# Three linear-attention loops rebuilt: v from TensorE into three PSUM banks, multiplied in place and scanned there

## The chip, the cores and the metric

The kernel runs on one core of a Trainium2 chip. The metric is the device time of one execution in microseconds (us), as the median of several runs; lower is better.

## The reference

A residual model of eight layers over x of 2048 tokens by 128 channels, all in f32: each layer adds its block's output to x, and each block works on the layer-normed x.

```
x = x + softmax_attention(norm(x))      # 16 heads of 8, causal, over 2048 tokens
x = x + channel_mix(norm(x))
x = x + gated_linear(norm(x))           # the three "linear" blocks
x = x + channel_mix(norm(x))
x = x + retention(norm(x))
x = x + experts(norm(x))                # top 2 of 8
x = x + lightning(norm(x))
x = x + experts(norm(x))
```

The three linear blocks have one form. For each head (16) and each pair (d, e) of its 8 by 8 state there is a recurrence over the tokens, and the output is a sum over d:

```
S[t] = a[t] * S[t-1] + k[t, d] * v[t, e]
o[t, e] = sum over d of q[t, d] * S[t]
```

In gated a is sigmoid(key) per channel and token, k is 1 - a, and the output goes through the matrix ho with a bias. In retention and lightning a is a constant per head; retention then normalises per head over time and multiplies by ro; lightning takes silu of q, k and v, normalises per token, multiplies by a gate (two small products and a sigmoid) and by lo.

## The kernel before

The stages run one after another: softmax_attention, channel_mix, linear_attention("gated"), channel_mix, linear_attention("retention"), experts, linear_attention("lightning"), experts. x stays in SBUF with tokens on partitions (16 tiles of 128); xT holds the normed and transposed x, channels on partitions.

**A linear stage** has 128 partitions for (head, d) and loops over n = 0..31: four chunks c of 512 tokens (NC, CH), and in each the eight values e (HD). A step n makes the row of v for e, replicated over d, in the layout (head, d) x 512; multiplies it by k (L1120, DVE) into one of four SBUF buffers upd; scans it (L1134, DVE) with the decay into a state buffer; multiplies the state by q (L1085, POOL) into z; and TensorE adds z into the output bank of the chunk (add_product, four steps later by LAG). In gated and lightning add_product uses z as the stationary operand, four 128-token tiles at a time, with reduce_w (L1229), and the output comes with tokens on partitions; for gated reduce_w is orep, the output matrix's rows replicated by eight DMAs, so that the output matrix is applied in the same product. In retention it is one product with pick stationary (L1224), and the output has channels on partitions.

The rows of v come in two ways. For all e of the first chunk and five of eight later, TensorE makes them (L1244) into one of two PSUM banks (4 and 5); in lightning ACT applies Silu in place (L1185). For e = 3, 5 and 7 of the later chunks (by_dma) TensorE makes the whole of v for the chunk once (L1250), ACT copies it (L1190), SP stores it to DRAM and loads it back replicated, and POOL multiplies it by k (L1090), three steps ahead. At step 5 of a chunk k and q of the next chunk are projected (L1213, two products). Lightning also makes a gate at steps 2 and 3 (L1256, L1259). DVE adds the finished chunk to x in gated (add: L1096, L1098 and the statistics L194) or takes statistics of y.

Each engine's queue runs in the order of the code; semaphores carry the dependencies.

**The softmax stage** has an order written out by a planner, attention_order, which counts time for each engine and yields PLAN. The maxima of the scores (DVE L720 over TensorE products L771 into a ring of two slots, banks 4 to 7) are computed ahead of the exponentials (ACT L841 over products L788 into three score banks 0 to 2) and the products with v (L802, bank 3). For each of the 16 steps (four heads, 512 queries) the maxima are turned (L824), copied to mrow (L733), and written by four small DMAs (set_maxima, L659) as rows of the stacked Q; the scores of that step wait for them. ACT issues these DMAs for the first four steps (EARLY), SP for the rest. SP also stores the bf16 parts of Q and K of each chunk to DRAM and loads them stacked (store, stack), chunks 2 and 3 right at the start of this block. A "fill" is a product into a free ring slot whose result is not used; the planner puts one in where PE would wait over 0.25 us by its count, if the ring slot is free.

## Time and profile before

| | |
|---|---|
| median of 3 runs | 1269.7 us (1269.53 to 1271.92) |
| profiled execution, its time | 1268.4 us |
| its span, first to last instruction | 1266.7 us |
| mean granted TensorE clock | 0.871 of full |
| busy: PE, DVE, ACT, POOL | 989.5, 873.5, 511.3, 479.7 us |

The profile is of one execution. PE is TensorE (PEld its weight loads), DVE VectorE, ACT ScalarE, POOL GpSimd, SP the queue that issues DMAs. L1134 is line 1134 of the kernel before. A busy PE is not a PE at its peak, as matmuls are pipelined. An f32 product shows as two MATMUL instructions. Idle time of an engine that is not the limit costs nothing, so the rows are read stage by stage.

### The profile page before, as it was taken

The page shows a single profiled execution, that of the slowest core. Times are in us where ns is not written, and L with a number is a line of the kernel's source. Part 1 is how long each engine was busy: PE and PEld are TensorE (multiplying, and loading weights), DVE is VectorE, ACT ScalarE, POOL GpSimd, SP SyncE. Part 2 cuts the span into 40 slices and gives each one's busy share as a digit, 9 for nine tenths or more (in the row PEclk, how much of TensorE's full clock was granted, in tenths as well). Part 3 has the DMA queues.
Part 4 walks back from the last instruction along what each step waited for, and adds up shares of the span by engine and source line. Part 5 has one row for each costly group of instructions (what it writes and reads, how often), then busy time and mean ns, then how long its engine had stood idle before and what let it go on. Part 6 is the DMA issues. An engine that isn't in the chain of part 4 may idle for free. (4 is left out here: it accounts for less than half of the span.)

```text
span 1266.7 us, 17452 instructions
## 1 busy us (share of the span) xinstructions
PE 989.5 (78%) x5892; PEld 500.1 (39%) x5892; DVE 873.5 (69%) x1502; ACT 511.3 (40%) x1048; POOL 479.7 (38%) x506
## 2 busy tenths in 40 slices
PE   5477899899999999686767775399984985369994
PEld 3222222222222333544453223166661544236663
DVE  6957889898988830889878985633337997643335
ACT  5234577687877776320021101033334321113333
POOL 2311110011101112248834883146642797136662
PEclk9657889899999999789868986599996997679997
DMA  6881000000000000511001101011112110101114
GB/s 134 175 192 19 1 1 1 1 1 2 1 1 1 2 3 7 193 58 51 9 1 33 51 17 33 13 32 42 43 37 75 59 34 1 34 21 42 43 43 116
DMA packets 50204, 51.45 MB, mean 41 GB/s; under 512 B 7668, under 2 KB 39804, under 8 KB 50108
## 3 DMA queue, kind: packets, MB, share of 16 engines
q1 hardware_dynamic: 44888, 40.06, 12.4%
q0 software_dynamic: 4992, 10.23, 3.0%
q8 instruction: 51, 0.84, 0.3%
q14 instruction: 33, 0.27, 0.1%
q10 hardware_dynamic: 240, 0.05, 0.0%
HBM read 33.22 MB, written 16.91 MB: 40 GB/s over the span
## 5 line engine op out<-in xcount | busy, mean ns | idle before, releaser
L720 DVE TENSOR_REDUCE mpart<-ps 128x2 f32<-128x1024 f32 (+3 forms) x320 | 325.3, 1061 | 59.4 <-PE ps L771 34.2
L841 ACT ACTIVATE arena<-ps 128x512 f32<-128x512 f32 (+3 forms) x640 | 292.1, 542 | 143.2 <-PE ps L788 133.9
L788 PE MATMUL ps<-arena 51*128 51x512 bf16 (+3 forms) x640 | 182.3, 372 | 14.9 <-ACT arena L841 6.2
L1085 POOL TENSOR_TENSOR arena<-arena 128x512 f32<-128x512 f32 x96 | 148.6, 1559 | 64.9 <-DVE arena L1134 63.7
L771 PE MATMUL ps<-arena 51*128 51x512 bf16 (+3 forms) x640 | 149.9, 383 | 21.2 <-DVE mpart L720 15.7
L802 PE MATMUL ps<-arena,w 128*32 128x512 f32 (+3 forms) x1280 | 160.5, 575 | 2.9 <-ACT arena L841 2.5
L690 POOL TENSOR_SCALAR_AFFINE_SELECT arena<-arena 128x512 f32<-128x512 f32 x64 | 40.6, 634 | 313.8 <-ACT arena L841 231.3
L1669 ACT ACTIVATE arena<-ps 128x512 f32<-128x512 f32 x78 | 46.6, 597 | 219.6 <-PE ps L1732 163.4
L1579 DVE COPY arena<-ps 128x128 f32<-128x128 f32 x78 | 22.8, 292 | 154.4 <-PE ps L1722 146.5
L1134 DVE TENSOR_TENSOR_SCAN arena<-cst,arena 128x512 f32<-128x512 f32 x64 | 124.0, 1959 | 2.0 <-POOL arena L1090 2.0
L788 PEld LDWEIGHTS ps<-arena 51*128 51x128 bf16 x640 | 50.2, 95 | 174.5 <-ACT arena L841 136.4
L1634 POOL DMA_INDIRECT results<-arena x78 | 76.8, 984 | 91.5 <-DVE arena L1596 77.2
L1623 POOL DMA_INDIRECT arena<-tokens,arena x78 | 75.7, 971 | 76.7 <-DVE arena L1572 53.5
L1731 PE MATMUL ps<-w,arena 128*128 x156 | 82.9, 614 | 2.9 <-DVE arena L1579 2.4
L1750 PE MATMUL ps<-w,arena 128*128 x624 | 82.7, 275 | 1.1 <-DVE arena L1596 1.1
L1732 PE MATMUL ps<-w,arena 128*128 x156 | 81.4, 604 | 0.0
L1750 PEld LDWEIGHTS ps<-w,arena 128*128 128x128 f32 x624 | 75.8, 192 | 1.6 <-issue 1.5
L1244 PE MATMUL ps<-xt,arena 128*128 128x512 f32 x138 | 72.7, 615 | 3.5 <-DVE arena L1120 3.4
L182 PE MATMUL ps<-cst,xn 128*128 128x128 f32 x96 | 22.5, 396 | 60.7 <-DVE xn L165 58.9
L173 POOL TENSOR_TENSOR small<-small,neghalf 128x4 f32<-128x4 f32 x32 | 32.4, 1050 | 96.2 <-DVE small L160 96.2
L1120 DVE TENSOR_TENSOR arena<-ps,arena 128x512 f32<-128x512 f32 x69 | 46.0, 667 | 28.9 <-PE ps L1244 19.2
L189 ACT COPY xt<-ps 128x512 f32<-128x512 f32 x28 | 16.2, 589 | 121.5 <-PE ps L182 121.4
(263 smaller groups left out, 1525.6 us busy)
## 6 DMA issues: line engine op xcount, KB each, us to landing
w<-in_w SPq DMA_DIRECT2D x2, 2048.0 KB, 11.4
arena<-results SPq DMA_DIRECT2D x16, 256.0 KB, 4.9
arena<-q_stack SPq DMA_DIRECT2D x8, 384.0 KB
arena<-k_stack SPq DMA_DIRECT2D x8, 384.0 KB
arena<-g_v SPq DMA_DIRECT2D x9, 256.0 KB
arena<-r_v SPq DMA_DIRECT2D x9, 256.0 KB, 3.6
arena<-l_v SPq DMA_DIRECT2D x9, 256.0 KB, 3.6
tokens<-arena SPq DMA_DIRECT2D x8, 256.0 KB, 2.4
```

The source lines that it names most:

```text
L720: nc.vector.tensor_reduce(out=mpart[:, 2 * pl:2 * pl + 2, t, kc], in_=ps[:, bank:bank + 2, 0:width], axis=AX.X, op=ALU.max).then_inc(ring_ ...
L771: ins = nc.tensor.matmul(ps[:, bank + side, 0:width], rows(Qs, side, 2 * g + pl, (c * TPC + t) * P, (c * TPC + t + 1) * P), rows(Ks, side, ...
L788: nc.tensor.matmul(ps[:, n % ST, off:CH], rows(Ks, j % 2, 2 * g + j // 2, kt * P, (kt + 1) * P), rows(Qs, j % 2, 2 * g + j // 2, c * CH + ...
L802: ins = nc.tensor.matmul(ps[32 * j:32 * j + 32, O, off:CH], vg[kt // (NT // 2)][:, kt % (NT // 2), g * GH + j, :], probs[:, u % 2, j, off: ...
L841: nc.scalar.activation(probs[:, n % 2, j[0], off:CH], ps[:, (GH * n + j[0]) % ST, off:CH], ACT.Exp, scale=float(HD) ** -0.5).then_inc(exp_ ...
L1085: nc.gpsimd.tensor_tensor(z[:, n % ZB, :], state[:, n % SB, :], q[:, c % 2, :], ALU.mult).then_inc(z_ready, 1)
L1134: nc.vector.tensor_tensor_scan(out=state[:, n % SB, :], data0=a, data1=upd[n % UB], initial=0.0 if c == 0 else state[:, (n - HD) % SB, CH ...
L1623: nc.gpsimd.indirect_dma_start(out=xs[:, s, :], out_offset=None, in_=token_rows, in_offset=bass.IndirectOffsetOnAxis(ap=gather_row[:, s:s ...
L1634: nc.gpsimd.indirect_dma_start(out=result_rows, out_offset=bass.IndirectOffsetOnAxis(ap=result_row[:, s:s + 1], axis=0), in_=y[:, s % YB, ...
L1731: nc.tensor.matmul(ps[:, i % 2, :], xsT[:, i % 2, :], w1[:, expert[i], :], start=True, stop=True)
L1732: nc.tensor.matmul(ps[:, 2 + i % 2, :], xsT[:, i % 2, :], w3[:, expert[i], :], start=True, stop=True).then_inc(up_ready, 1)
L1750: ins = nc.tensor.matmul(ps[:, 7, 0:D], hidT[:, s % 2, f, :], w2[:, expert[s], f, :], start=f == 0, stop=f == NF - 1)
```

## The change

In the linear stages all rows of v are made by TensorE, into three PSUM banks (4, 5, 0). DVE multiplies by k in place in the bank, and the scan reads its input from the bank. The way over DRAM, POOL's updates, orep and the upd buffers are gone. The sum over d is one product with pick stationary in all three kinds, with channels on partitions; in gated and lightning ACT copies the chunk's sum (copy_inner), TensorE turns it to tokens on partitions (outer: with ho as the moving operand in gated, as transposes in lightning), into the same bank, and in lightning ACT copies it again (copy_outer). In gated the add moves from step 5 to step 7. Norm uses banks 1 and 7.

In the softmax stage SP issues all row DMAs; store and stack of chunks 2 and 3 come after the rows of steps 1 and 3 have landed; and the planner also puts fills into a free score bank.

```diff
@@ attention_order
-                while can[what][0] - pe > 0.25 and free <= pe:
+                n = GH * su + sj
+                bank_free = n < GH * NU and (n < 3 or exp_end[n - 3] + 0.06 <= pe) if n < 3 or len(exp_end) > n - 3 else False
+                while can[what][0] - pe > 0.25 and (free <= pe or bank_free):
...
-                    plan.append(("fill", slots))
+                    plan.append(("fill", slots) if free <= pe else ("fill scores", n))
@@ softmax_attention, sync
                         stack(sp, 1)
-                        for c in (2, 3):
-                            store(sp, c)
-                            stack(sp, c)
-                        for k in range(EARLY, NS):
+                        for k in range(NS):
                             set_maxima(sp, k)
+                            if k in (1, 3):
+                                c = (k + 3) // 2
+                                for j in range(GH):
+                                    sp.wait_ge(max_set[j], 16 * (k + 1))
+                                store(sp, c)
+                                stack(sp, c)
@@ softmax_attention, tensor
+                        def fill_scores(n):
+                            if n >= ST:
+                                pe.wait_ge(exp_done, n - ST + 1)
+                            nc.tensor.matmul(ps[:, n % ST, 0:320], identb[:], cstb[:, 0:320], start=True, stop=True)
@@ softmax_attention, scalar
-                            if what == "turn max" and n < EARLY:
-                                set_maxima(act, n)
@@ linear_attention
-            norm = Norm(name, x, xn, NT, 1e-5)
+            norm = Norm(name, x, xn, NT, 1e-5, banks=(1, 7))
+            def v_bank(n):
+                return ps[:, (4, 5, 0)[n % 3], :]
@@ gpsimd
-                        if n + 3 in by_pool:
...
-                            nc.gpsimd.tensor_tensor(upd[u % UB], vd[:, m % VB, :], k[:, u // HD % 2, :], ALU.mult).then_inc(upd_pooled, 1)
@@ vector
-                        nc.vector.tensor_tensor(upd[n % UB], v_in, k[:, n // HD % 2, :], ALU.mult).then_inc(upd_ready, 1)
+                        nc.vector.tensor_tensor(v_bank(n), v_bank(n), k[:, n // HD % 2, :], ALU.mult).then_inc(upd_ready, 1)
...
-                            out=state[:, n % SB, :], data0=a, data1=upd[n % UB],
+                            out=state[:, n % SB, :], data0=a, data1=v_bank(n),
...
-                        if kind == "gated" and c >= 1 and n % HD == LAG + 1:
+                        if kind == "gated" and c >= 1 and n % HD == HD - 1:
                             add(dve, c - 1)
@@ scalar
+                def copy_inner(act, c):
                     act.wait_ge(z_used, (c + 1) * HD)
+                    if kind == "retention":
+                        nc.scalar.copy(y[:, c * CH:(c + 1) * CH], ps[:, 6 + c % 2, :]).then_inc(sum_out, 1)
+                    else:
+                        if c >= 2:
+                            act.wait_ge(outer_ready, c - 1)
+                        nc.scalar.copy(inner[:, c % 2, :], ps[:, 6 + c % 2, :]).then_inc(inner_out, 1)
+                def copy_outer(act, c):
+                    act.wait_ge(outer_ready, c + 1)
                     nc.scalar.copy(y[:, c * CH:(c + 1) * CH], ps[:, 6 + c % 2, :]).then_inc(sum_out, 1)
...
-                            nc.scalar.activation(dec[:, c % 2, :], pk, ACT.Sigmoid, bias=col["key_b"])
...
-                            nc.scalar.activation(k[:, c % 2, :], pk, ACT.Sigmoid, bias=negb, scale=-1.0).then_inc(kq_out, 1)
+                            nc.scalar.activation(k[:, c % 2, :], pk, ACT.Sigmoid, bias=negb, scale=-1.0)
+                            nc.scalar.activation(dec[:, c % 2, :], pk, ACT.Sigmoid, bias=col["key_b"]).then_inc(kq_out, 1)
@@ tensor
+                        nc.tensor.matmul(ps[:, 6 + c % 2, :], pick[:, e, :], z[:, n % ZB, :], start=e == 0,
+                                         stop=e == HD - 1).then_inc(z_used, 1)
+                    def outer(c):
+                        pe.wait_ge(inner_out, c + 1)
+                        for t in range(TPC):
+                            out, tile = ps[:, 6 + c % 2, t * P:(t + 1) * P], inner[:, c % 2, t * P:(t + 1) * P]
+                            if kind == "gated":
+                                ins = nc.tensor.matmul(out, tile, w["ho"][:], start=True, stop=True)
+                            else:
+                                ins = nc.tensor.transpose(out, tile, ident)
+                        ins.then_inc(outer_ready, 1)
...
+                        if n >= 3:
+                            pe.wait_ge(scanned, n - 2)
+                        nc.tensor.matmul(v_bank(n), vrep[:, e].rearrange("p h d -> p (h d)"),
+                                         xT[:, c * CH:(c + 1) * CH], start=True, stop=True).then_inc(v_ready, 1)
...
+                        if e == LAG + 2 and c >= 1 and kind != "retention":
+                            outer(c - 1)
```

## Rows read from the trace of the kernel before

**Rows 1.** Windows, the three loops: busy us (instructions) per engine, PE clock, DMA share, GB/s
```profile
550.40:635.80 85.40, 65.26 (x302) 43.43 (x301) 78.92 (x70) 7.16 (x12) 63.20 (x40) 0.91 0.12 37
680.70:763.40 82.70, 63.31 (x121) 23.30 (x120) 75.79 (x58) 7.10 (x12) 64.89 (x40) 0.89 0.13 39
976.90:1059.20 82.30, 68.26 (x317) 41.76 (x315) 76.76 (x67) 24.33 (x42) 66.76 (x40) 0.96 0.13 39
```

**Rows 2.** Timeline of DVE: start, us, line, idle before; start and end of retention's loop
```profile
609.22 0.84 DVE L194 BATCH_NORM_STATS2 stats<-x 128x6 f32<-128x128 f32 x4
...
682.13 1.21 DVE L1134 TENSOR_TENSOR_SCAN arena<-cst,arena 128x512 f32<-128x512 f32 x1
683.26 0.67 DVE L1120 TENSOR_TENSOR arena<-ps,arena 128x512 f32<-128x512 f32 x1
683.85 1.92 DVE L1134 TENSOR_TENSOR_SCAN arena<-cst,arena 128x512 f32<-128x512 f32 x1
...
761.17 2.27 DVE L1134 TENSOR_TENSOR_SCAN arena<-cst,arena 128x512 f32<-128x512 f32 x1 [0.51 <-POOL arena L1090]
768.10 0.69 DVE L1106 BATCH_NORM_STATS2 stats<-arena 128x6 f32<-128x512 f32 x1 [4.67 <-ACT arena L1150]
```

**Rows 3.** Timeline of POOL, the same stretch
```profile
683.43 1.27 POOL L1085 TENSOR_TENSOR arena<-arena 128x512 f32<-128x512 f32 x1 [5.13 <-DVE arena L1134]
```

**Rows 4.** Instructions of one line: duration ns min/median/max, first and last start
```profile
L1120 DVE TENSOR_TENSOR arena<-ps,arena x69: 658/659/693, 550.4 to 1050.3; 128x512 f32<-128x512 f32 x69
...
L1098 DVE TENSOR_TENSOR x<-x,out_bias x4: 691/844/1446, 586.6 to 641.3; 128x512 f32<-128x512 f32 x4
```

**Rows 5.** Timeline of PE, products back to back in gated and in retention
```profile
561.56 1.02 PE L1244 MATMUL ps<-xt,arena 128*128 128x512 f32 x2
...
562.43 1.05 PE L1229 MATMUL ps<-arena 128*128 128x128 f32 x8
...
687.44 1.02 PE L1224 MATMUL ps<-arena,cst 128*128 128x512 f32 x2
688.29 1.02 PE L1213 MATMUL ps<-xt,w_rk 128*128 128x512 f32 x2
```

**Rows 6.** Timeline, hand-over from DVE to PE (gated), from PE to ACT (lightning)
```profile
562.74 0.66 DVE L1120 TENSOR_TENSOR arena<-ps,arena 128x512 f32<-128x512 f32 x1
...
563.46 1.12 PE L1244 MATMUL ps<-xt,arena 128*128 128x512 f32 x2
...
983.70 1.02 PE L1244 MATMUL ps<-xt,arena 128*128 128x512 f32 x2
...
984.76 0.58 ACT L1185 ACTIVATE ps<-ps 128x512 f32<-128x512 f32 x1 [1.17 <-PE ps L1244]
```

**Rows 7.** Timeline of ACT, the issues of the second set of rows
```profile
76.05 3.07 ACTq L659 DMA_DIRECT2D arena<-mrow  x4
79.22 2.13 ACT L841 ACTIVATE arena<-ps 128x256 f32<-128x256 f32 x8 [4.95 <-issue]
```

**Rows 8.** Timelines: SP, first store and last stack issue of chunk 2; DVE, fourth set
```profile
57.69 4.27 SPq L375 DMA_DIRECT2D q_stack<-w  x6
...
72.53 0.62 SPq L383 DMA_DIRECT2D arena<-k_stack  x1
...
118.92 0.18 DVE L726 TENSOR_REDUCE negmax<-mpart 128x16 f32<-128x32 f32 x1
```

**Rows 9.** Windows in the softmax stage, columns as in rows 1
```profile
50.00:100.00 50.00, 33.54 (x276) 12.72 (x274) 34.12 (x47) 15.00 (x38) 7.48 (x20) 0.59 0.87 185
100.00:115.00 15.00, 12.88 (x82) 3.71 (x80) 11.35 (x14) 5.83 (x12) 0.00 (x0) 0.54 0.00 1
...
125.00:135.00 10.00, 8.26 (x56) 2.33 (x56) 5.78 (x6) 6.18 (x16) 1.27 (x2) 0.66 0.00 1
...
170.00:220.00 50.00, 46.85 (x390) 14.30 (x386) 46.34 (x47) 37.41 (x83) 5.86 (x12) 1.00 0.01 2
```

**Rows 10.** Window in gated's loop, columns as in rows 1
```profile
575.00:580.00 5.00, 1.88 (x10) 1.79 (x10) 5.00 (x4) 0.00 (x0) 5.00 (x3) 0.87 0.22 56
```

More of the change, by code:

```diff
@@ L1010, in linear_attention @@
             k = take(2 * CH).rearrange("p (b t) -> p b t", b=2)
-            spare = take(2 * CH)
-            dec = spare.rearrange("p (b t) -> p b t", b=2)
-            upd = take(2 * CH)
             SB, ZB = HD + 4, HD
@@ L1018, in linear_attention @@
             vrep = take(HD * P).rearrange("p (e h d) -> p e h d", e=HD, h=H)
-            orep = take(HD * P).rearrange("p (e m) -> p e m", e=HD)
+            inner = take(2 * CH).rearrange("p (b t) -> p b t", b=2)
             y = take(T)
@@ L1023, in linear_attention @@
             g1 = low_rank[0:HD, :].rearrange("p (b t) -> p b t", b=2)
-            UB = 4
-            upd = [half[:, i * CH:(i + 1) * CH] for half in (upd, low_rank if kind == "gated" else spare) for i in (0, 1)]
             negb = take(1)
-            VB = 4
-            vd = take(VB * CH).rearrange("p (b t) -> p b t", b=VB)
-            v_full = xn[:, 0:2 * TPC, :].rearrange("p (b t) d -> p b (t d)", b=2)
-            v_dram = nc.dram_tensor(name + "_v", [NC, P, CH], FP32, kind="Internal").ap()
-            by_dma = [n for n in range(NC * HD) if n >= HD and n % HD in (3, 5, 7)]
-            by_pe = [n for n in range(NC * HD) if n not in by_dma]
-            by_pool, by_dve = by_dma, by_pe
-            v_full_ready = sem(name + "_v_full_ready")
-            v_full_out = sem(name + "_v_full_out")
-            v_stored = sem(name + "_v_stored")
-            v_loaded = [sem(f"{name}_v_loaded{b}") for b in range(VB)]
-            norm = Norm(name, x, xn, NT, 1e-5)
+            norm = Norm(name, x, xn, NT, 1e-5, banks=(1, 7))
+            dec = take(2 * CH).rearrange("p (b t) -> p b t", b=2)
+            def v_bank(n):
+                return ps[:, (4, 5, 0)[n % 3], :]
             rep_ready = sem(name + "_rep_ready")
```

104 lines of the change are left out of this document (25 added, 79 removed).

## Prediction

> **What bounds the kernel now.** I read the page's busy shares first; no engine is full over the whole span, so the question is which one is full in each stage. The table of windows gives it. In the softmax stage's steady part, 170 to 220 us, PE is busy 46.9 and DVE 46.3 of 50 us [rows 9]; in the loops of the three linear stages DVE is busy 78.9 of 85.4, 75.8 of 82.7 and 76.8 of 82.3 us [rows 1]. The change rewrites these loops, 250.4 us together; it also edits the softmax stage.
>
> Then the timeline of DVE in the loop of retention [rows 2]. The first scan, with POOL idle, takes 1.21 us (1.13 to the next start); from the second on a scan takes 1.92. The reader is to see why: the multiply at 683.26 gives way to a scan at 683.85, but POOL's first z product runs from 683.43 to 684.70 [rows 3], and from 684.70 the scan needs its 1.1 us more, to 685.77. So a scan (two SBUF inputs) stands still while POOL's product (two SBUF inputs) runs, and one step costs 0.58 + 1.85 = 2.43 us. The multiply L1120, with one input in PSUM, takes 658 to 693 ns in all 69 cases, beside POOL or not [rows 4]. L1098, with both inputs in SBUF, goes from 691 to 1446 ns. That is the pattern on which the whole forecast rests: only an operation of DVE with two SBUF inputs is held by POOL, and the scan's held part is 0.7 us, 96 times.
>
> PE's timeline gives the next limit. One 128x512 f32 product is two instructions and keeps PE for 0.87 us (561.56 to 562.43) or 0.85 us (687.44 to 688.29) at full clock [rows 5].
>
> **The change, part by part.**
>
> *Scan from PSUM.* Its data1 moves to PSUM, so one SBUF input stays (dec or the constant). By the pattern it takes 1.13 start to start; with the 0.59 of the multiply a step is 1.73 instead of 2.43. No row shows a scan that reads PSUM, nor a DVE write into PSUM. Bounds: nothing extra (the multiply's read from PSUM costs no more than L1098's free 691 ns), or 0.3 us a step for both instructions together, half of a multiply again, an estimate at the far end. I take nothing, as the multiply is the nearest row; 0.3 would be 29 us over 96 steps. The Trainium skill ("VectorE: DVE Perf Modes", section on the TRN2 errata) speaks against this: it gives a VectorE instruction from PSUM 62 cycles more than one from SBUF. By that the scans alone would add about 6 us; the rows of L1120 and L1098 do not show it.
>
> *POOL without the updates.* Three products in eight from the second chunk on leave POOL. Its z product (1.27 us) then fits into 1.73, so POOL's lag, for which the last scan waited, goes. Eight rows of v by PE in place of five, no copy of v to DRAM and back, no ACT copy of v: off the path, except that PE gets the work.
>
> *PE becomes the neighbour limit.* Per step it does one product for v and one for the sum: 2 x 0.86 = 1.72 us, against DVE's 1.73. Its extras therefore show: k and q (1.72 per chunk, three chunks), in gated the four final products (8 instructions, 0.9), in lightning the two gate products (1.72) and four transposes (0.6, estimate). The slack: from a bank's release to its next multiply is 0.06 (563.40 to 563.46) + 1.12 + 0.04 (984.72 to 984.76, to ACT) = 1.22 us [rows 6], and three banks allow 1.73, so 0.5 us of PE's lateness is free. In lightning ACT's Silu stands between: PE start to Silu start 1.06, Silu 0.58 [rows 6], so the chain is 0.16 + 1.06 + 0.58 + 0.04 = 1.84 us (0.16: the release and the 0.1 that a waiting product takes longer). The multiply n waits for the scan n-3 by this chain and the scan n-1 follows it after 1.73, so two steps take at least 1.84 + 1.73, one 1.78.
>
> Chunks of eight steps, 13.8 us by DVE:
> - Retention: first chunk 13.8 + (1.72 - 0.5) = 15.0; the middle two also the statistics (0.6) = 15.6; last 14.4 (no k and q). Sum 60.6 against 82.7: minus 22.1.
> - Gated: the add of a chunk is DVE time (0.66 + 0.69 + 0.8 of statistics [rows 2, 4] = 2.15). First 15.0; middle: between PE's sum 13.8 + 2.6 = 16.4 and all extras in a row 18.3, I take 17.2; last 16.4. Sum 65.8 against 85.4: minus 19.6.
> - Lightning: PE bound, 20 products x 0.86 + 0.6 = 17.8, with 0.3 of friction 18.1 in the middle, 17.4 first, 16.4 last. Sum 70.0 against 82.3: minus 12.3.
>
> *Tails.* Retention: from the last scan's end to the last statistics is 768.79 - 763.44 = 5.4 us now, as POOL is three products behind; afterwards 0.1 + 1.27 (z, [rows 3]), 1.18 (sum), 0.63 (ACT's copy, as the Silu), 0.7 (statistics): 3.9. Minus 1.4. Gated and lightning gain as much and lose most of it to the added turn: a copy, and four products or transposes with a second copy (1.2 to 1.9 us, less the 8 small matmuls that one matmul pair replaces). I take 0.5 each. Together minus 2.4.
>
> Sum of the linear stages: 22.1 + 19.6 + 12.3 + 2.4 = 56.4 us. Bounds: by DVE alone (62, 57, 58 us) 76; with scans still held by POOL (2.43 a step) only the removed waits, 9.
>
> *Order of k and dec, Norm's banks, the loads of orep*: the two sigmoids come as a pair either way; banks 1 and 7 are free then; orep loads beside the norm. Nothing on the path; without that cover it would be one sigmoid, some 0.7 us.
>
> *Softmax stage: row DMAs from SP.* Now ACT issues the first four sets. 76.05 to 79.12 it issues four DMAs, its exponentials start at 79.22 after 4.95 us without work [rows 7], and PE and DVE wait with it. These sixteen issues move to SP. Behind SP's new waits stand store and stack of chunks 2 and 3 (28 DMAs): chunk 2's maxima are first wanted after the fourth set is reduced, at 119.1 us; its store can start once the second set has landed, near 80, and store and stack take SP 57.69 to 73.15 = 15.5 us [rows 8], with landing some 20. That is 19 us of cover, about 10 when the stage runs faster. In exchange the small row loads no longer share the queues with the bulk stores. DVE is busy 34.1 of 50 us between 50 and 100, against 46.3 at 170 to 220 [rows 9]: at most 12 us to win. I take 6.
>
> *Fills into the score banks.* At 100 to 115 and 125 to 135 PE's clock is at 0.54 and 0.66, that is largely at 1.2 GHz, after gaps in its work; by the 0.927 share of 170 to 220 DVE lost 2.6 and 3.5 us there [rows 9], and two such stretches follow before 235. Fills keep PE at work in such gaps. Some 10 us are at stake, part of it the ACT gaps; I take 4. None, or plus 3 if fills stand in front of maxima, is the other end. The planner's order may shift with them; I keep it as neutral.
>
> Sum: 1268.4 (profiled, its span 1266.7 and 1.7 around it) - 56.4 - 6 - 4 = 1202.0. The median of the runs is 1.3 above the profiled time: **1203 us**.
>
> **Rivals.**
> - *PSUM is dearer for DVE* (0.3 us a step): 1203 + 29 = 1232. Against it: 658 ns of L1120. For it: no row shows a PSUM write by DVE or a scan from PSUM. Chance 0.14.
> - *The scan stays held by POOL*: it writes SBUF, reads dec or the constant and its start value from SBUF. Then the linear stages give 9, in all 1203 + 47 = 1250. Against it: L1120 writes SBUF too and is never held. The Trainium skill ("SBUF — State Buffer", section Who interferes with whom) says that a DVE instruction with at most one SBUF input outside the two-port modes doesn't contend; by that this rival is out. Chance 0.08.
> - *The softmax stage gives nothing or loses*, since chunk 2's stack comes late or fills stand in the way: 1213 to 1216. Chance 0.10.
> - *The other side: PE at 1.2 GHz in the loops.* Its waits between banks let the clock fall, as between 575 and 580 us, where PE had 1.88 us of work in 5 and the clock was 0.87 [rows 10]. At 1.2 GHz a step is 4 x 0.86 = 3.44 us, PE bound, 1.7 more than 1.73. It outweighs all the gain when 66 / 1.7 = 39 of the 96 steps run so; with 45 the time is 1279. Against it: PE would be 99% loaded, and at 170 to 220, with 46.9 of 50 busy, the clock is 1.00. Chance 0.06.
> - The forecast: 0.62.
>
> **How the numbers follow.** A measurement of this kernel tells about 0.2% from no change. All cases but the last end more than 0.2% below 1269.7: faster 0.93, same 0.01, slower 0.06. The likeliest case's own range is 1185 to 1218 (linear stages 45 to 65, softmax 3 to 18). The range asked for must reach the dearer PSUM case and stays short of the held scan: 1182 to 1236.
>
> **What the profile will show.** Right: scans near 1.2 us beside a running POOL; a DVE step of 1.7 to 1.8; PE near 100% at clock 1.0 in the loops, and DVE's waits now for the v product at the fifth to sixth step of each chunk; in lightning waits for ACT's Silu; loops of about 61, 66 and 70 us; no ACT issue gap near 76 us, and fills between 100 and 240. Wrong: scans of 1.9 (held), multiplies over 0.75 (PSUM write), PE clock under 0.8 in the loops, DVE waiting for a stack DMA near 110 us. Most of my risk is in the PE extras: if they overlap DVE's slack better than I count, gated and lightning gain up to 10 us more.

## The result, and the profile after it

The changed kernel takes 1202.2 us (median of 4 runs, 1197.0 to 1205.2) against 1269.6 us (1267.3 to 1271.9) before; the ratio is 0.9465, 95% interval [0.9424, 0.9506]. It is faster by 5.3%. The forecast was 1203 us. The profiled execution took 1200.0 us, its span is 1198.2 us (before 1266.7).

Each stage's norm begins with the same DVE instruction, so its starts split the 68.5 us of span that went: up to the first channel mix 513.2 became 497.8 (minus 15.4), the gated stage 102.8 became 84.0 (minus 18.8), retention with its own norm 111.6 became 90.3 (minus 21.3), lightning up to its output norm 100.2 became 87.7 (minus 12.5), and the rest, mixes and experts, gave 0.5. So the linear stages brought 52.6 us, where the forecast had 56.4, and the softmax stage 15.4, where it had 10.

The windows of the three loops in the changed kernel, from the first multiply to the end of the last scan (they answer to [rows 1]):

```profile
533.90:601.10 67.20, 61.70 (x158) 27.13 (x158) 60.92 (x73) 7.08 (x13) 39.18 (x31) 1.00 0.00 1
646.40:709.00 62.60, 59.74 (x135) 24.35 (x136) 58.43 (x67) 5.32 (x9) 39.35 (x31) 1.00 0.00 1
919.90:991.30 71.40, 69.52 (x162) 26.22 (x160) 59.84 (x73) 29.30 (x51) 39.17 (x31) 1.00 0.00 0
```

DVE's busy time fell from 78.9, 75.8 and 76.8 us to 60.9, 58.4 and 59.8, and POOL's from 63 to 67 to 39. PE is now busy 92, 95 and 97% of the loops, and its granted clock is 1.00 in all three: the rival with the slow clock did not come.

The start of retention's loop, the timelines of DVE and then of POOL (they answer to [rows 2, 3]):

```profile
648.09 1.21 DVE L1112 TENSOR_TENSOR_SCAN arena<-cst,ps 128x512 f32<-128x512 f32 x1
649.21 0.67 DVE L1098 TENSOR_TENSOR ps<-ps,arena 128x512 f32<-128x512 f32 x1
649.80 1.21 DVE L1112 TENSOR_TENSOR_SCAN arena<-cst,ps 128x512 f32<-128x512 f32 x1
```

```profile
649.38 1.27 POOL L1072 TENSOR_TENSOR arena<-arena 128x512 f32<-128x512 f32 x1 [5.62 <-DVE arena L1112]
```

POOL's z product runs from 649.38 to 650.65, over most of the scan that starts at 649.80. In the kernel before, that scan took 1.92 us; here it takes 1.21, as the one before it with POOL idle. A step is 649.80 - 648.09 = 1.71 us in the first chunk. The groups of instructions, with shapes kept apart, give the means for the whole kernel:

```profile
L1098 DVE TENSOR_TENSOR ps<-ps,arena 128x512 f32<-128x512 f32 x96 | 65.6, 684 | 33.0 <-PE ps L1229 17.2 <-ACT ps L1171 15.6
L1112 DVE TENSOR_TENSOR_SCAN arena<-cst,arena,ps 128x512 f32<-128x512 f32 x48 | 60.9, 1271 | 0.0
L1112 DVE TENSOR_TENSOR_SCAN arena<-arena,ps 128x512 f32<-128x512 f32 x32 | 40.0, 1254 | 0.0
```

The multiply that writes into PSUM takes 684 ns on the mean (before 667, into SBUF). A scan has one of two lengths: 1.21 in the first chunk, 1.27 from the second on, where its start value is a column of the state and not 0.0. And 33 us of idle time stand before the multiplies, 17.2 behind the v product of PE and 15.6 behind ACT's Silu. What was DVE's own time before is now in part waiting for its neighbours. One such wait in retention, on DVE and on PE:

```profile
686.48 1.27 DVE L1112 TENSOR_TENSOR_SCAN arena<-cst,arena,ps 128x512 f32<-128x512 f32 x1
688.86 0.70 DVE L1098 TENSOR_TENSOR ps<-ps,arena 128x512 f32<-128x512 f32 x1 [1.11 <-PE ps L1229]
```

```profile
686.08 1.02 PE L1196 MATMUL ps<-xt,w_rk 128*128 128x512 f32 x2
686.94 1.02 PE L1196 MATMUL ps<-xt,w_rq 128*128 128x512 f32 x2
687.80 1.02 PE L1229 MATMUL ps<-xt,arena 128*128 128x512 f32 x2
```

The projections of k and q keep PE for 687.80 - 686.08 = 1.72 us; the v product behind them is late, and DVE waits 1.11 us. Retention has such a wait in each of three chunks (1.31, 1.34, 1.11 us). The gated loop has the same three, two more of 0.73 behind the outer products, and smaller ones, 6.2 us together. Lightning has fifteen waits for the Silu, 11.4 us together. These are 21.8 of the 33.0 us; the other 11.1 stand ahead of the three loops (3.4, 3.5 and 4.3), where DVE waits for the first row of v.

The softmax stage, by windows (they answer to [rows 9]; the last takes in the rest of the stage, which in the kernel before had DVE 254.7 and a clock of 0.95):

```profile
50.00:100.00 50.00, 38.44 (x353) 16.36 (x353) 38.77 (x53) 13.76 (x36) 7.53 (x20) 0.84 0.63 128
100.00:115.00 15.00, 13.86 (x94) 4.04 (x96) 10.46 (x11) 10.61 (x21) 0.07 (x1) 0.74 0.01 1
125.00:135.00 10.00, 9.58 (x79) 3.02 (x77) 8.61 (x10) 8.32 (x17) 0.95 (x2) 1.00 0.66 157
170.00:220.00 50.00, 45.97 (x369) 15.27 (x369) 46.93 (x51) 30.87 (x70) 6.73 (x16) 1.00 0.01 2
160.00:450.00 290.00, 275.22 (x2260) 86.44 (x2257) 249.39 (x272) 219.21 (x469) 30.94 (x79) 0.99 0.01 2
```

The clock in the first three of these windows is higher than before (0.84, 0.74 and 1.00 against 0.59, 0.54 and 0.66), and DVE does 38.8 us of its work between 50 and 100 instead of 34.1. ACT has no issues and no 4.95 us hole at 76 us any more. But there is a new hole, on PE. The timeline of SP, and of PE:

```profile
88.44 0.60 SPq L385 DMA_DIRECT2D arena<-q_stack  x1
...
92.21 27.94 SPq L660 DMA_DIRECT2D arena<-mrow  x8
```

```profile
94.93 0.31 PE L819 MATMUL ps<-cstb,identb 128*128 128x320 bf16 x1
100.83 1.03 PE L792 MATMUL ps<-arena 51*128 51x512 bf16 x3 [5.58 <-DMA arena<-mrow]
```

SP issues the four loads of chunk 2's stack from 88.44 on (384 KB each), and the small rows of set 2 right behind them, from 92.21 on (the line takes set 3's in as well). PE waits 5.58 us for these rows, and the window after the hole is the one with the clock at 0.74.

### The profile page after: what moved, and what is told of

Read it like the earlier page. It is cut to its first block and busy times, and to the rows that moved or that the text cites. A ratio compares the mean times of both kernels' runs of the same rounds, so it can differ in the third digit from the quotient of the medians.

```text
span 1198.2 us, 17070 instructions
## 1 busy us (share of the span) xinstructions
PE 979.1 (82%) x5703; PEld 468.7 (39%) x5703; DVE 823.8 (69%) x1529; ACT 514.6 (43%) x1056; POOL 400.7 (33%) x479
## 5 line engine op out<-in xcount | busy, mean ns | idle before, releaser
L792 PE MATMUL ps<-arena 51*128 51x512 bf16 (+3 forms) x640 | 175.0, 356 | 13.3 <-DMA arena<-mrow 6.0
L806 PE MATMUL ps<-arena,w 128*32 128x512 f32 (+3 forms) x1280 | 153.4, 551 | 2.7 <-ACT arena L852 2.2
L1072 POOL TENSOR_TENSOR arena<-arena 128x512 f32<-128x512 f32 x96 | 121.8, 1269 | 91.9 <-DVE arena L1112 85.1
L775 PE MATMUL ps<-arena 51*128 51x512 bf16 (+3 forms) x640 | 140.8, 359 | 12.9 <-DVE mpart L724 5.8
L1598 POOL DMA_INDIRECT results<-arena x78 | 77.0, 987 | 90.5 <-DVE arena L1560 77.1
L1229 PE MATMUL ps<-xt,arena 128*128 128x512 f32 x192 | 99.9, 604 | 8.1 <-DVE arena L1112 7.3
L1204 PE MATMUL ps<-arena,cst 128*128 128x512 f32 x192 | 98.8, 599 | 3.6 <-POOL arena L1072 3.3
L1098 DVE TENSOR_TENSOR ps<-ps,arena 128x512 f32<-128x512 f32 x96 | 65.6, 684 | 33.0 <-PE ps L1229 17.2
L1714 PEld LDWEIGHTS ps<-w,arena 128*128 128x128 f32 x624 | 75.8, 192 | 1.5 <-issue 1.5
L182 PE MATMUL ps<-cst,xn 128*128 128x128 f32 x96 | 22.3, 393 | 60.9 <-DVE xn L165 59.2
L1112 DVE TENSOR_TENSOR_SCAN arena<-cst,arena,ps 128x512 f32<-128x512 f32 x48 | 60.9, 1271 | 0.0
## 6 DMA issues: line engine op xcount, KB each, us to landing
w<-in_w SPq DMA_DIRECT2D x2, 2048.0 KB, 11.1
```

Of the source, the lines that this page charges most:

```text
L775: ins = nc.tensor.matmul(ps[:, bank + side, 0:width], rows(Qs, side, 2 * g + pl, (c * TPC + t) * P, (c * TPC + t + 1) * P), rows(Ks, side, ...
L792: nc.tensor.matmul(ps[:, n % ST, off:CH], rows(Ks, j % 2, 2 * g + j // 2, kt * P, (kt + 1) * P), rows(Qs, j % 2, 2 * g + j // 2, c * CH + ...
L806: ins = nc.tensor.matmul(ps[32 * j:32 * j + 32, O, off:CH], vg[kt // (NT // 2)][:, kt % (NT // 2), g * GH + j, :], probs[:, u % 2, j, off: ...
L1072: nc.gpsimd.tensor_tensor(z[:, n % ZB, :], state[:, n % SB, :], q[:, c % 2, :], ALU.mult).then_inc(z_ready, 1)
L1204: nc.tensor.matmul(ps[:, 6 + c % 2, :], pick[:, e, :], z[:, n % ZB, :], start=e == 0, stop=e == HD - 1).then_inc(z_used, 1)
L1229: nc.tensor.matmul(v_bank(n), vrep[:, e].rearrange("p h d -> p (h d)"), xT[:, c * CH:(c + 1) * CH], start=True, stop=True).then_inc(v_read ...
```

## The experiments

All ran beside the kernel before. Where two experiments are compared, I use the loops (first multiply to end of the last scan) of their profiles: in kernels with the changed loops these agree within 0.15 us where the code of a loop is the same and the clock is 1.00. The start of the first channel mix does not: nine kernels with the same softmax code as the changed one (497.8) have it between 493.6 and 500.0 us, one profile of each. So a start of the mix is good to about 3 us, and totals that differ by less say little by themselves.

### The softmax part alone

The linear stages are those of the kernel before; only the edits to the planner, the fills, the row DMAs and the order of store and stack are made.

> The kernel before with the softmax part of the change alone (fills in the score banks, all row DMAs on SP, stores and stacks put between them); the linear stages are those of before. Theory: the two parts don't touch each other, so the first channel mix begins at 498 us as in the changed kernel instead of 513, and everything after it stays as it was: 1254 us, 15 under before. Rival: part of the gain ahead of the mix is owed to something else, or is paid back later: 1260 to 1270.

Measured: 1252.6 us, ratio 0.9849 [0.9834, 0.9864]; the mix begins at 498.2, and the loops are 85.4, 82.0 and 83.4 us where they were 85.4, 82.8 and 82.3: retention 0.8 shorter, lightning 1.1 longer. That goes with PE's mean clock in these windows, 0.95 and 0.91 against 0.89 and 0.96 in the kernel before. Otherwise the two halves of the change are independent. The softmax part is worth 18.3 us in the median here, 13.2 in the span of the profiled execution (the slowest of the four), 15 at the mix.

### Which part of the softmax edits

Without the fills in the score banks:

```diff
-                while can[what][0] - pe > 0.25 and (free <= pe or bank_free):
+                while can[what][0] - pe > 0.25 and free <= pe:
```

> The changed kernel without the fills in the score banks; the row DMAs stay on SP in the new order. Theory: the granted clock of TensorE in the stretch 50 to 115 us of the softmax rises from 0.59 to 0.84 by these fills, and this is worth about half of the 15 us: the first channel mix begins at 504 to 507 us, the whole takes 1208 to 1211. Rival 1: the order of the row DMAs alone brings the 15 us (mix at 498, 1202). Rival 2: the fills bring it all (mix at 513, 1217).

Measured: 1211.3 us, ratio 0.9527 [0.9514, 0.9540]; the mix begins at 507.9. Windows of this kernel:

```profile
50.00:100.00 50.00, 31.20 (x299) 13.14 (x299) 38.90 (x54) 14.22 (x37) 7.49 (x20) 0.67 0.66 129
125.00:135.00 10.00, 9.71 (x78) 3.03 (x77) 8.60 (x9) 8.51 (x19) 0.64 (x1) 1.00 0.58 157
160.00:450.00 290.00, 271.80 (x2202) 84.13 (x2198) 253.41 (x275) 215.66 (x457) 29.10 (x76) 0.94 0.01 2
```

With the fills but the row DMAs as before:

```diff
                         stack(sp, 1)
-                        for k in range(NS):
-                            set_maxima(sp, k)
-                            if k in (1, 3):
...
+                        for c in (2, 3):
+                            store(sp, c)
+                            stack(sp, c)
+                        for k in range(EARLY, NS):
+                            set_maxima(sp, k)
...
+                            if what == "turn max" and n < EARLY:
+                                set_maxima(act, n)
```

> The changed kernel with the fills in the score banks, but with the row DMAs issued as before: sets 0 to 3 by ACT, stores and stacks first on SP. Theory: the rows by SP are worth the other half: mix at 505 to 508 us instead of 498, the whole 1209 to 1212. Rival 1: all by the order of the rows (mix at 513, 1217). Rival 2: all by the fills (mix at 498, 1202).

Measured: 1211.0 us, ratio 0.9533 [0.9520, 0.9546]; the mix begins at 504.8. Windows of this kernel:

```profile
50.00:100.00 50.00, 38.84 (x307) 15.15 (x307) 32.20 (x43) 13.94 (x36) 7.05 (x18) 0.70 0.92 189
125.00:135.00 10.00, 9.66 (x66) 2.89 (x66) 6.29 (x7) 6.20 (x15) 1.23 (x2) 0.50 0.01 2
160.00:450.00 290.00, 275.04 (x2279) 86.45 (x2278) 256.14 (x279) 221.18 (x469) 29.24 (x76) 0.99 0.01 2
```

So the order of the rows alone brings 513.2 - 507.9 = 5.3 us at the mix and the fills alone 8.4; together they bring 15.4. Both rivals are out: neither part alone reaches the changed kernel's start of the mix, and neither gives nothing. How much each is worth is less sure than the decimals say. Taken out of the changed kernel, the fills cost 10.1 us at the mix and the rows 7.0; in the medians of the runs they cost 9.1 and 8.8. The windows show the division of labour: with the rows on SP, DVE gets 38.9 us of work done between 50 and 100, with or without fills (32.2 without the rows); the fills hold the clock at 0.99 from 160 to 450, with the rows on SP or on ACT, where it is 0.94 without them (0.95 in the kernel before). Not every window with a low clock was the fills' to mend: between 125 and 135 us the clock is 1.00 with the new rows and no fills, and 0.50 with the fills and the old rows.

### The new hole at 95 us

```diff
                                 store(sp, c)
-                                stack(sp, c)
+                            if k in (2, 4):
+                                stack(sp, k // 2 + 1)
```

> The changed kernel with each stack load on SP moved behind the row DMAs of the next set: store, rows of the next set, stack, instead of store, stack, rows. In the changed kernel TensorE waits 5.6 us at 95 to 101 us for the rows of set 2, which were issued at 92.2 right behind the stack load (88.4 to 91.0) and landed at about 100.8. Theory: the rows land in about 3 us once the bulk isn't ahead of them, the hole shrinks to under 2 us, and the mix begins 3 to 5 us earlier: 1197 to 1199. Rival: the stack load is then late for set 4 by as much, or the hole only moves to the next set: 1202, mix at 497 to 499.

Measured: 1203.2 us, ratio 0.9471 [0.9450, 0.9491]; the mix begins at 501.0, no better than in the changed kernel. The waits of PE between 85 and 115 us in this kernel (total, times, longest):

```profile
PE ps L776 <- DMA arena<-k_stack: 3.6, 1, 3.6
...
PE ps L793 <- DMA arena<-mrow: 0.2, 1, 0.2
```

The mechanism is as the theory had it: the rows, issued from 96.23 on, were there when PE wanted them at 99.2. The Trainium skill ("DMA: Bandwidth & Descriptors", section Queues, rings and completion order) says that each DMA engine consumes a ring's descriptors in the order in which they were put there; the wait that goes with the bulk load ahead of the rows agrees. But the gain is not there: the stack load is now late for chunk 2 by 3.6 us, and clock and work between 115 and 125 us fall. The rival was right. Both transfers are wanted at the same time, and their order decides which one PE waits for; waiting of 3.8 us in place of 5.6 would not be seen in a start of the mix that is good to 3 us.

### The scan's input back in SBUF

```diff
+            upd = take(3 * CH).rearrange("p (b t) -> p b t", b=3)
...
+                        if n >= 3:
+                            dve.wait_ge(scanned, n - 2)
-                        nc.vector.tensor_tensor(v_bank(n), v_bank(n), k[:, n // HD % 2, :], ALU.mult).then_inc(upd_ready, 1)
+                        nc.vector.tensor_tensor(upd[:, n % 3, :], v_bank(n), k[:, n // HD % 2, :], ALU.mult).then_inc(upd_ready, 1)
...
-                            out=state[:, n % SB, :], data0=a, data1=v_bank(n),
+                            out=state[:, n % SB, :], data0=a, data1=upd[:, n % 3, :],
...
-                            pe.wait_ge(scanned, n - 2)
+                            pe.wait_ge(upd_ready, n - 2)
```

> The changed kernel with one thing undone: the multiply writes its product into three buffers in SBUF and the scan reads it from there; all v products stay on TensorE, in the three PSUM banks, which come free after the multiply. Theory: the scan then has both inputs in SBUF and is held while POOL's z product runs: it takes 1.9 us instead of 1.27 on the mean, the step of a channel 2.4 instead of 1.77, the three loops 86, 83 and 84 us instead of 67, 63 and 71, the whole 1240 to 1250. Rival: the place of the scan's input doesn't matter, the gain came from POOL's and SP's work that left the loops; then the step stays at 1.77 and the whole at 1202, or below, since the banks come free earlier.

Measured: 1241.4 us, ratio 0.9763 [0.9745, 0.9780]; the loops take 79.8, 78.1 and 77.1 us. Timeline of DVE in retention, and of POOL beside it:

```profile
681.91 1.92 DVE L1115 TENSOR_TENSOR_SCAN arena<-cst,arena 128x512 f32<-128x512 f32 x1
683.75 0.66 DVE L1101 TENSOR_TENSOR arena<-ps,arena 128x512 f32<-128x512 f32 x1
684.33 1.93 DVE L1115 TENSOR_TENSOR_SCAN arena<-cst,arena 128x512 f32<-128x512 f32 x1
```

```profile
683.91 1.27 POOL L1073 TENSOR_TENSOR arena<-arena 128x512 f32<-128x512 f32 x1 [1.16 <-DVE arena L1115]
```

The step is back at 684.33 - 681.91 = 2.42 us, and the scans take 1.85 us on the mean. The edit also frees a bank earlier, after the multiply and not after the scan, which can only help. So this one operand brings back 33.7 us in the loops and 8.6 outside them (in gated DVE waits 4.0 us for the last outer product instead of 1.5): 42.3 of the 52.6 us that the linear stages gained (39.2 in the medians of the runs). The loops were expected at 86, 83 and 84 us, as long as in the kernel before, and are 5 to 7 us shorter. The other 10 of the 52.6 us come from the rest of the rewrite, among it no updates on POOL and no rows of v through DRAM; its parts but the sums by channels (below) were not tried one by one.

### The same without POOL's product

In that kernel POOL's `state * q` is replaced by a copy of 8 columns, and PE sums the state; the multiplication by q is left out.

```diff
-                        nc.gpsimd.tensor_tensor(z[:, n % ZB, :], state[:, n % SB, :], q[:, c % 2, :], ALU.mult).then_inc(z_ready, 1)
+                        nc.gpsimd.tensor_copy(z[:, n % ZB, 0:8], state[:, n % SB, 0:8]).then_inc(z_ready, 1)
```

> The kernel with the multiply into SBUF (scan with both inputs in SBUF), and POOL's product state x q left out: POOL copies 8 columns in its place and TensorE sums the state itself. It leaves out the multiplication by q. Theory: what made the scan 1.85 us instead of 1.27 was POOL's 1.27 us product beside it; without it the scan takes 1.21 to 1.27 with its inputs in SBUF too, the step 1.8 and the retention loop about 62. Rival: the scan is simply slower when its second input comes from SBUF: it stays at 1.85 and the loop at 78.

Measured: 1191.7 us in one run; the loops take 62.9, 59.9 and 69.2 us. The groups of instructions in this kernel:

```profile
L1115 DVE TENSOR_TENSOR_SCAN arena<-cst,arena 128x512 f32<-128x512 f32 x64 | 80.8, 1263 | 0.0
L1115 DVE TENSOR_TENSOR_SCAN arena<-arena 128x512 f32<-128x512 f32 x32 | 40.3, 1263 | 0.0
```

With both tensor inputs in SBUF and no product on POOL the scan takes 1.26 us; with POOL's product beside it 1.85; with one input in PSUM 1.27 or less, product or not. That settles it: the scan pays for two SBUF inputs only beside POOL's product, and reading PSUM costs it nothing that these means show. The Trainium skill ("VectorE: DVE Perf Modes", section on the TRN2 errata) would have put 62 cycles more on each instruction with a PSUM source than on one with an SBUF source; these means don't show them. The Trainium skill's rule on the shared port ("SBUF — State Buffer", section Who interferes with whom) is that a DVE instruction with two SBUF inputs contends with a GpSimd instruction that reads SBUF, and one with at most one does not; all three times agree with it.

The changed kernel has one DVE instruction in its loops that still reads two tensors from SBUF, the add of the output bias in gated (L1080). Once a product of POOL falls on it, and once not:

```profile
567.55 1.28 DVE L1080 TENSOR_TENSOR x<-x,out_bias 128x512 f32<-128x512 f32 x1
586.45 0.69 DVE L1080 TENSOR_TENSOR x<-x,out_bias 128x512 f32<-128x512 f32 x1
```

```profile
567.01 1.27 POOL L1072 TENSOR_TENSOR arena<-arena 128x512 f32<-128x512 f32 x1 [0.50 <-DVE arena L1112]
585.14 1.27 POOL L1072 TENSOR_TENSOR arena<-arena 128x512 f32<-128x512 f32 x1 [0.50 <-DVE arena L1112]
```

The first add begins 0.54 us into POOL's product and takes 0.59 us longer than the second, which begins 0.04 us after a product has ended. With POOL's product gone all four adds take 0.69.

### What makes PE late: k and q

The projections of k and q for chunks 1 to 3, and ACT's copies of them, are left out; chunk 0's are used for all.

```diff
-                        if e == LAG + 1 and c + 1 < NC:
-                            project_kq(c + 1)
...
-                        if e == LAG + 1 and c + 1 < NC:
-                            take_kq(c + 1)
```

> The changed kernel without the projections of k and q (and of the gated stage's decay) for chunks 1 to 3: chunk 0's are used for all. It leaves these products and ACT's copies of them out. Theory: the 1.1 to 1.3 us waits at the sixth channel of a chunk come from these two products (1.72 us of TensorE) ahead of v's; without them the retention loop falls from 62.7 to 57 to 58 us (8 steps of 1.71, 24 of 1.77, the statistics), lightning from 71.4 to 66 to 67, gated from 67.3 to 62 to 63. Rival: TensorE is late with v for another reason (the fixed order with the sums, or the three banks) and the loops shorten by less than 1.5 us each.

Measured: 1189.8 us in one run. The windows of the loops in this kernel:

```profile
534.50:596.50 62.00, 56.69 (x146) 24.30 (x146) 60.65 (x73) 1.76 (x3) 39.24 (x31) 1.00 0.00 1
641.00:699.60 58.60, 55.30 (x123) 21.13 (x124) 58.14 (x67) 1.76 (x3) 39.37 (x31) 1.00 0.00 1
913.50:980.50 67.00, 65.11 (x149) 23.58 (x148) 59.79 (x73) 25.71 (x45) 39.15 (x31) 1.00 0.00 0
```

The loops fall by 5.3, 4.1 and 4.4 us (67.3 to 62.0, 62.7 to 58.6, 71.4 to 67.0). In retention DVE is now busy 58.14 of 58.60 us: with these products gone, DVE alone sets the loop. Its three waits (1.31, 1.34, 1.11 us) are gone. The steps in which they lay, from one scan's start to the next, were 3.12, 3.22 and 2.99 us and are 1.71, 1.77 and 1.77 now: 4.1 us together, 0.1 more for each than the wait alone. The six products are 5.2 us of PE's time in each loop; in gated all of it was on the path, in the other two some four fifths. Retention's 58.6 lies above the 57 to 58 that was expected.

### The carry

Every scan starts from 0.0; the carry from chunk to chunk is left out.

```diff
-                            initial=0.0 if c == 0 else state[:, (n - HD) % SB, CH - 1:CH],
+                            initial=0.0,
```

> The changed kernel with every scan started from 0.0 instead of the last column of the state (the carry from chunk to chunk is left out). Theory: the start value read from SBUF is what makes the scans of chunks 1 to 3 1.27 instead of 1.21 us; with 0.0 all 96 take 1.21, the step is 1.71 throughout and the retention loop shortens by up to 24 x 0.06 = 1.4 us. Since TensorE needs 2 x 0.86 = 1.72 us for each channel, part of it may turn into waits: 0.4 to 1.4 in each loop. Rival: the length has to do with the later chunks, not with the start value (POOL and ACT beside it): the scans stay at 1.27.

Measured: 1201.2 us in one run; the loops take 66.5, 63.3 and 71.2 us. The groups of instructions in this kernel:

```profile
L1112 DVE TENSOR_TENSOR_SCAN arena<-cst,ps 128x512 f32<-128x512 f32 x64 | 77.4, 1210 | 0.0
L1098 DVE TENSOR_TENSOR ps<-ps,arena 128x512 f32<-128x512 f32 x96 | 65.9, 686 | 37.2 <-PE ps L1229 20.7 <-ACT ps L1171 16.2
```

The start value read from SBUF is the cause of the 0.06 us. But the loops did not shorten as expected: minus 0.74, plus 0.65 and minus 0.17. The scans save 4.3 us in all and the waits before the multiplies grow by 4.2 (33.0 to 37.2). With 1.71 a step DVE is faster than PE's two products (1.72), and what it saves it waits. That retention even got longer has another cause, PE's clock. The window, and the timelines of PE and DVE in it:

```profile
649.40:652.80 3.40, 3.40 (x5) 1.35 (x4) 3.03 (x4) 0.00 (x0) 2.24 (x3) 0.50 0.01 2
```

```profile
650.53 1.91 PE L1204 MATMUL ps<-arena,cst 128*128 128x512 f32 x2
```

```profile
653.60 0.70 DVE L1098 TENSOR_TENSOR ps<-ps,arena 128x512 f32<-128x512 f32 x1 [1.00 <-PE ps L1229]
```

For 3.4 us the granted clock is 0.50, the level of 1.2 GHz, and the product takes 1.91 us instead of 1.02. DVE waits 1.00 and, one step earlier, 0.16 us for the late v products, in places where the changed kernel has no wait. PE had waited 1.14 and 0.61 us for banks just before, but so it had in the changed kernel, where the clock stayed at 1.00. What makes it fall in the one and not in the other is not shown; it is the forecast's rival of the slow clock, in small.

### One bank more

```diff
+            VBANKS = (4, 5, 0) if kind == "lightning" else (4, 5, 0, 1)
+            VB = len(VBANKS)
...
-                return ps[:, (4, 5, 0)[n % 3], :]
+                return ps[:, VBANKS[n % VB], :]
...
-                        if n >= 3:
-                            pe.wait_ge(scanned, n - 2)
+                        if n >= VB:
+                            pe.wait_ge(scanned, n - VB + 1)
```

> The changed kernel with a fourth PSUM bank for v (bank 1, which the norm has left) in the gated and retention stages; lightning unchanged. Theory: the stalls of 1.1 to 1.3 us at the sixth channel of each chunk come from TensorE, which is late with v by the projections of k and q (1.72 us) because it may run only three banks ahead; one bank more hides them: gated loop 67.3 to about 63, retention 62.7 to about 60, the whole 1196 to 1198. Rival: TensorE has no slack over the chunk as a whole (2 x 0.86 us for each channel against a step of 1.77, plus 1.72 per chunk), so it can't run ahead and a fourth bank stays empty: loops within 0.5 us of the three banks', 1202.

Measured: 1198.9 us, ratio 0.9433 [0.9419, 0.9447]; the gated loop takes 64.3 and retention 60.8 us (67.3 and 62.7 with three banks), lightning the same 71.4. The gain is 3.0 and 1.8 us, of 4.3 and 2.7 expected, and the whole stays above the expected 1196 to 1198. Of retention's three waits two are left, on the timeline of DVE:

```profile
664.68 0.70 DVE L1101 TENSOR_TENSOR ps<-ps,arena 128x512 f32<-128x512 f32 x1 [1.34 <-PE ps L1232]
680.13 0.70 DVE L1101 TENSOR_TENSOR ps<-ps,arena 128x512 f32<-128x512 f32 x1 [0.59 <-PE ps L1232]
```

A bank gives PE one more head start of a step, once; in a middle chunk PE's own work (8 x 1.72 + 1.72 = 15.5 us) is longer than DVE's, so PE can't earn it back. The first expectation held in its direction, the rival in its reason.

### The sums as before

z is the stationary operand again in gated and lightning, in four tiles; the inner copy and the second product are gone.

```diff
-                        nc.tensor.matmul(ps[:, 6 + c % 2, :], pick[:, e, :], z[:, n % ZB, :], start=e == 0,
-                                         stop=e == HD - 1).then_inc(z_used, 1)
+                            for t in range(TPC):
+                                ins = nc.tensor.matmul(ps[:, 6 + c % 2, t * P:(t + 1) * P], z[:, n % ZB, t * P:(t + 1) * P],
+                                                       reduce_w[:, e, :], start=(e, t) == (0, 0), stop=(e, t) == (HD - 1, TPC - 1))
...
-                        if e == LAG + 2 and c >= 1 and kind != "retention":
-                            outer(c - 1)
```

> The changed kernel with the sums by channels undone in the gated and lightning stages: z is the stationary operand again, in four tiles, against the repeated output weights (gated, loaded by 8 DMAs) or the picking matrix (lightning), so that no inner copy and no second product is needed. Theory: TensorE's extra work in these loops is what delays v after the projections; without it the gated loop loses about 1 us per chunk and the tails 1 to 2 us: 1196 to 1199. Rival: the four small products for each channel cost TensorE more than they save (four of 128 columns with a weight load each instead of one of 512): the two stages get longer by 2 to 6 us, 1204 to 1208.

Measured: 1197.1 us, ratio 0.9415 [0.9401, 0.9428]; the gated loop takes 65.6 us (67.3) and lightning's 70.9 (71.4), and the gated stage as a whole is 3.4 us shorter (80.6 against 84.0), half of that behind the loop. So the sums by channels, one of the edits of the change, cost time in gated: 3.4 us. Lightning's stage is 0.7 us shorter too (87.0 against 87.7), but in four kernels with the changed code for it that stage takes 87.3 to 88.6 us, so only the loop's 0.5 counts there. In the medians of the runs the edit is worth 5.1 us.

### The Silu of v left out

```diff
-                        if kind == "lightning":
-                            act.wait_ge(v_ready, n + 1)
-                            nc.scalar.activation(v_bank(n), v_bank(n), ACT.Silu).then_inc(v_out, 1)
```

> The changed kernel with the Silu of v left out in the lightning stage, so VectorE multiplies k with the raw product. Theory: the hand-over from TensorE to ACT to VectorE and back (three banks, about 1.73 + 1.84 us for a round of two) costs lightning 1 us per chunk over what TensorE's own work asks (16 products of 0.86 + gate 1.72 + projections 1.72 + transposes 0.6 = 17.8 us); without it the chunk takes 17.8 instead of 18.5 and the loop 69 instead of 71.4. Rival 1: the chain is the whole of it and the chunk falls to the 15.9 of the retention loop: loop 64. Rival 2: TensorE alone sets it: 71.

Measured: 1200.5 us, ratio 0.9437 [0.9421, 0.9453]; lightning's loop takes 69.3 us instead of 71.4. Its window in this kernel:

```profile
923.70:993.00 69.30, 68.59 (x162) 27.19 (x162) 59.28 (x73) 11.75 (x20) 39.17 (x31) 1.00 0.00 0
```

PE is busy 68.6 of 69.3 us. So PE's work sets lightning, and the chain through ACT adds the 2.1 us on top; the waits that the profile puts down to ACT are for the most part PE's lateness, passed on.

### Both gains together

The sums as before, and the fourth bank.

> The changed kernel with the two edits that each gained: the sums by channels undone in gated and lightning (z as stationary operand), and the fourth PSUM bank for v in gated and retention. Theory: the tokens form takes 0.9 us of TensorE's work out of each gated chunk and shortens the tail, the bank hides what is left of TensorE's lateness: gated loop 62 to 63 us (67.3 in the changed kernel, 65.6 and 64.3 with one edit each), retention 60.8, lightning 70.9; the sum of both gains is 9 us: 1192 to 1194. Rival: both edits remove the same stalls and the gains don't add: gated loop 64, the whole 1195 to 1197.

Measured: 1193.9 us (1188.9 to 1197.3, 5 runs), ratio 0.9390 [0.9364, 0.9416]. The windows of its loops:

```profile
535.20:598.00 62.80, 60.45 (x315) 40.35 (x314) 60.66 (x73) 5.22 (x9) 39.20 (x31) 1.00 0.00 1
641.60:702.40 60.80, 59.08 (x135) 25.12 (x136) 58.43 (x67) 5.31 (x9) 39.30 (x31) 1.00 0.00 1
915.00:986.00 71.00, 69.45 (x330) 42.23 (x328) 59.78 (x73) 27.79 (x49) 39.10 (x31) 1.00 0.00 1
```

The loops take 62.7, 60.8 and 71.0 us, as expected for all three. The gated loop gains 4.5 us where the single edits gave 1.7 and 3.0: the gains add. It is faster than the kernel before by 6.1%, and its linear stages are 8.5 us shorter than in the changed one.

## Why the prediction was right, step by step

- **The scan is held by POOL, and a PSUM input frees it.** Right, and shown both ways: the input back in SBUF makes the scan 1.85 us, and POOL's product taken away makes it 1.26. The step was forecast at 1.73 us and is 1.71 in the first chunk and 1.77 later. Nothing for PSUM was the right value of the unknown price for the scan; the multiply that writes PSUM costs 17 ns more.
- **PE becomes the neighbour limit, and its extras show.** Right: the waits come at the k and q products, and without those products the loops lose 5.3, 4.1 and 4.4 us.
- **The sizes of the loops** were 65.8, 60.6 and 70.0 us and came out at 67.3, 62.7 and 71.4, 4.9 us too small together. For retention the rows say where: 8 x 1.71 + 24 x 1.77 = 56.2 us of steps instead of 55.4 counted at 1.73, and waits of 4.17 (0.41, 1.31, 1.34, 1.11) instead of the 3.7 of my three times 1.22. The other 0.5 is in the steps at the four waits, 0.1 longer each than the wait itself, and in the last scan, which counts with its full 1.27. The terms that were mis-sized are these; in the rows of before the 0.06 was hidden under POOL's 0.7. The carry's 0.06 is real but, as the run without it shows, removing it gives nothing while PE needs 1.72 for a step. In gated my middle chunk of 17.2 us, between the two bounds, came out at 18.1 (560.67 to 578.80), near the bound with all extras in a row, which I gave as 18.3 (13.8 + 2.15 + 2.6 is 18.55): DVE's adds and PE's outer product don't hide each other. And I counted the bias add with its free 0.69 us, though it keeps two SBUF inputs and the row of before reached 1446 ns; beside POOL it took 1.28 in this chunk.
- **The tails** were forecast at minus 2.4 us and came to that: 0.25 in gated, 1.5 in retention, 0.7 in lightning. The start of the stages gave 1.0 more, which I had left out.
- **The softmax stage** was undersized, 10 against 15.4 us. I split it as 6 for the rows and 4 for the fills. Alone they are worth 5.3 and 8.4, and on top of the other part 504.8 - 497.8 = 7.0 and 507.9 - 497.8 = 10.1. The term that was mis-sized is the fills': I saw 10 us at stake in the windows with a low clock, held part of them for the doing of ACT's gaps and took 4. Part of it was indeed the rows' (the clock of 1.00 between 125 and 135 without fills). The two stretches before 235 us were the fills': between 155 and 170 and between 220 and 235 the clock went from 0.66 to 1.00, and without fills it is 0.78 and 0.68. With a start of the mix that is good to 3 us, the split itself stays rough.
- **What is late next** was only half seen. I named a stack DMA that might come late; what came late were the rows behind it, 5.6 us at 95 us, and the run with the other order shows that these two trade places at a cost that can't be told apart.
- **The sum** of 1202.0 against 1200.0 profiled is better than its terms, and that is luck: 3.8 us too much for the linear stages, 5.4 too little for the softmax stage, 0.5 for mixes and experts. The rivals with dearer PSUM, with the held scan and with the slow clock are refuted for this kernel by the first windows and rows above, and the one with a softmax stage that gives nothing by its run alone.

## What to carry to other kernels

Before moving work away from a full engine, look whether its instructions are longer than the same ones with the neighbour idle: here 0.7 of each scan's 1.9 us was there only beside POOL's product, and changing where one operand lives took it away, while the rest of the rewrite was worth a fifth of what the linear stages gained. When the first limit goes, count the next engine's work for a whole period and not for a step: two products of 0.86 us against a step of 1.73 looked balanced, and nearly every extra product then went straight to the time. And test each edit of a change alone: the sums by channels cost 4 us or so inside a change that gained 67.

## What the hardware showed that was not expected

A scan whose start value is a column in SBUF takes 1.27 us for 512 columns against 1.21 with 0.0; taking the column away makes it 1.21 at once. The scan with one input in PSUM is no slower than with both in SBUF and POOL without its product (1.26 and 1.25 us over all four chunks against 1.26), and a multiply in place in PSUM takes 684 ns against 667 into SBUF. And the softmax stage doesn't repeat as the loops do: in ten kernels with the same code for it, the rows of set 2 are issued between 91.0 and 96.7 us, PE waits up to 6.0 us for them, and the mix begins between 493.6 (the four banks, where PE doesn't wait for them at all) and 500.0. The wait goes with how closely the rows follow the stack's loads on SP: 5.6 us where 3.8 us lie between the two first issues (the changed kernel), 4.8 at 4.8 us (no Silu), 1.7 at 7.7 us (no product on POOL) and none at 9.2 us (four banks). What sets that distance, I did not try.
